# Attention and mixture of experts in one kernel: gate weights and the shared expert's last rows in one stationary, the top two marked in place, part of the residual on other engines

## The reference, cut to what matters

```python
xn = layernorm(x)                                  # x: 16 x 256 x 128
# attention, per sequence
w = exp(tanh(((xn @ W + b) @ xn.T) / (|i - j| + 1e-7)))   # diagonal set to zero
attn = (w / (sum(w, -1) + 1e-7)) @ xn
# experts, per token: 8 experts, 2 taken, hidden size 176
scores = sigmoid(xn @ gate_w.T)
_, sel = top_k(scores + expert_bias, 2)
# routed input is xn * score of the expert taken
routed = sum over sel of square(relu(score * xn @ w_up[e].T)) @ w_down[e].T
shared = square(relu(xn @ shared_w_up.T)) @ shared_w_down.T
out = x + attn + routed + shared
```

## Time and profile before

| what | value |
|---|---|
| time, median of 3 runs | 129.37 us (129.23 to 129.52) |
| the profiled execution | 129.49 us, of which the span from first to last instruction is 127.6 |
| TensorE, matmul / weight load | 116.4 us (91%) / 84.6 us (66%), 960 instructions each |
| VectorE | 109.9 us (86%), 331 instructions |
| ScalarE | 82.5 us (65%), 106 instructions |
| GpSimd | 63.8 us (50%), 114 instructions |
| chain that ended last | PE 79%, DVE 11%, DMA 3%, issue 2%, ACT 2%, POOL 1% |
| granted TensorE clock | 0.993 over the span, 1.00 in every round |

### The profile page before, as it was taken

One profiled execution on the slowest core, in us unless ns is written; L12 is line 12 of the kernel. 1 busy time (PEld: TensorE's weight loads), 2 busy tenths in 40 slices (PEclk: granted clock), 3 DMA queues, 4 the chain that ended last, 5 costly groups with the idle time before them and its releaser, 6 DMA issues.

```text
span 127.6 us, 2805 instructions
## 1 busy us (share of the span) xinstructions
PE 116.4 (91%) x960; PEld 84.6 (66%) x960; DVE 109.9 (86%) x331; ACT 82.5 (65%) x106; POOL 63.8 (50%) x114
## 2 busy tenths in 40 slices
PE   3977787789999999999999999999999999999961
PEld 3954255457757884778567875778477856667951
DVE  5796898989999999999999999999999699968511
ACT  1226577688488927893689647983789378966400
POOL 5339719974954386437743695339643004431000
PEclk9999999999999999999999999999999999999997
DMA  3998003976666494559756866686768955698681
GB/s 86 386 406 322 12 0 43 156 145 113 113 113 116 133 177 86 99 129 115 143 97 115 189 113 113 118 181 128 99 122 133 149 107 98 155 147 169 129 213 65
DMA packets 49260, 17.65 MB, mean 138 GB/s; under 512 B 46432, under 2 KB 47200, under 8 KB 49248
## 3 DMA queue, kind: packets, MB, share of 16 engines
q1 hardware_dynamic: 48672, 15.83, 61.9%
q10 hardware_dynamic: 576, 1.66, 3.5%
HBM read 3.85 MB, written 2.10 MB: 47 GB/s over the span
## 4 chain that ended last, share of the span: by engine, by line
PE 79%; DVE 11%; DMA 3%; issue 2%; ACT 2%; POOL 1%; POOLq 0%; ACTq 0%
PE h_ps L633 14%; PE out_ps L659 12%; PE dots L587 10%; PE side L604 10%; DVE gated L467 6%; PE out_ps L651 6%; PE side L616 4%; PE small L579 4%; PE out_ps L666 4%; PE out_ps L648 4%; PE small L560 3%; DMA hiddenT<-hidden 3%; PE side L621 3%; PE small L568 2%; DVE resid L479 1%
## 5 line engine op out<-in xcount | busy, mean ns | idle before, releaser
L341 ACT ACTIVATE hidden<-gated 128x1408 bf16<-128x1408 bf16 x32 | 43.9, 1376 | 17.3 <-DVE gated L467 17.3
L467 DVE SCALAR_TENSOR_TENSOR gated<-h_ps,gates 128x1408 bf16<-128x1408 f32 x32 | 51.6, 1613 | 3.2 <-PE h_ps L633 3.2
L633 PE MATMUL h_ps<-upT,xnTb 128*128 128x512 bf16 (+1 forms) x96 | 24.3, 362 | 1.5 <-DVE gated L467 1.5
L225 POOL TENSOR_SCALAR xn<-x_sb,meanvar,rstd 128x128 f32<-128x128 f32 x28 | 22.0, 800 | 0.6
L659 PEld LDWEIGHTS out_ps<-downT,hiddenT 128*128 128x128 bf16 x308 | 19.4, 98 | 3.3
L659 PE MATMUL out_ps<-downT,hiddenT 128*128 128x128 bf16 x308 | 21.4, 219 | 0.0
L258 POOL TENSOR_TENSOR shidden<-srelu 128x512 f32<-128x512 f32 (+1 forms) x16 | 13.2, 828 | 15.4 <-ACT srelu L335 15.3
L251 POOL TENSOR_SCALAR_AFFINE_SELECT probs<-probs 128x256 f32<-128x256 f32 x16 | 6.6, 410 | 26.2 <-ACT probs L329 26.2
L587 PE MATMUL dots<-projT,xnT 128*128 128x256 f32 x60 | 16.4, 396 | 1.7 <-ACT projT L320 1.5
L604 PE MATMUL side<-xn,probs 128*128 128x129 f32 x128 | 17.0, 275 | 0.6 <-DVE resid L479 0.6
L604 PEld LDWEIGHTS side<-xn,probs 128*128 128x128 f32 x128 | 16.0, 192 | 2.1 <-issue 1.3
(11 more groups left out here) (84 smaller groups left out, 152.1 us busy)
## 6 DMA issues: line engine op xcount, KB each, us to landing
x_sb<-in_x SPq DMA_DIRECT2D x7, 256.0 KB, 9.1
out_y<-final SPq DMA_DIRECT2D x7, 256.0 KB, 2.6
up_raw<-in_up ACTq DMA_DIRECT2D x1, 704.0 KB, 7.0
down_raw<-in_down ACTq DMA_DIRECT2D x1, 704.0 KB, 9.0
hiddenT<-hidden SPq DMA_TRANSPOSE x32, 3.5
out_y<-final SPq DMA_DIRECT2D x2, 128.0 KB, 1.9
late_sb<-in_late SPq DMA_DIRECT2D x1, 224.0 KB, 7.1
x_sb<-in_x ACTq DMA_DIRECT2D x1, 128.0 KB, 2.8
```

Of the source, the lines that this page charges most:

```text
L225: g.tensor_scalar(xn[:, c, t, 0:D], x_sb[:, c, t, :], meanvar[:, c % 2, t, 0:1], rstd[:, c % 2, t:t + 1], ALU.subtract, ALU.mult).then_inc ...
L341: a.activation(hidden[:, t, :], gated[:, t, :], ACT.Square).then_inc(squared, 1)
L467: v.scalar_tensor_tensor(out=gated[:, t, :].rearrange("p (e h) -> p e h", e=E), in0=h_ps[:, 0:NH].rearrange("p (e h) -> p e h", e=E), scal ...
L633: last = t_.matmul(h_ps[:, at:to], xnTb[:, c % 4, t * P:(t + 1) * P], upT[:, at:to], start=True, stop=True)
```

## The change

- The gate's 8 columns and the shared expert's last 48 rows of weights stand together in one 64-column stationary, `restT`. `rest(f)` multiplies it in two matmuls with 256 tokens each, in the place of `logits(f)`; `shared_tail` is gone. Rows 0 to 7 and 64 to 71 of the result are logits, the 48 behind each are the tail of the shared expert of the front chunk.
- ScalarE takes exp of all rows (256 columns, its scale a column `gate_sign` that is -1 in the logits' rows and 0 elsewhere), then relu of the same rows (`relu_rest`); GpSimd squares that (`square_rest`). `transpose_exp` makes two transposes and also waits for the relu; in chunk 0 it writes to `h_ps`, so the first up-projection waits until they are read.
- The top two: the two largest values are copied to `pair`, whose other places hold a large negative number; `match_replace` writes a mark where the biased scores equal one of them; one operation on VectorE compares with the mark and multiplies by the scores. `max_index`, the two comparisons, GpSimd's two products and the table of expert numbers are gone.
- The residual of each chunk's first sequence: ScalarE scales attention by its norm (`scale_attention`), GpSimd adds x (`add_x`). The second sequence's stays on VectorE.
- Orders: on TensorE `up_tile(c,2)` stands ahead of `down_tile(o,1)`; on VectorE the sums, the norm, the statistics and the routing are interleaved anew; on ScalarE and GpSimd the new steps stand as in the diff. Semaphores count accordingly.
- The transfer of early constants has 32 columns more, that of late ones 64 fewer.

```diff
-W_AT, GATE_AT, B_AT, EB_AT, EARLY = 0, D, D + 32, D + 33, D + 33 + E
-SUP_AT, SDOWN_AT, STAIL_AT, LATE = 0, 192, 192 + D, 192 + D + D
+W_AT, REST_AT, B_AT, EB_AT, EARLY = 0, D, D + 64, D + 65, D + 65 + E
+SUP_AT, SDOWN_AT, STAIL_AT, LATE = 0, P, P + D, P + D + D
...
+        expneg = sb("expneg", [P, S])
...
+        def exp_bank(c):
+            return small[:, S:2 * S] if c else h_ps[:, 0:S]
...
-            def make_gates(c):
-                pool.wait_ge(match_ready, c + 1)
-                g.tensor_tensor(chosen[:, :, :], match[:, 0, :, :], match[:, 1, :, :], ALU.add).then_inc(gate_step, 1)
-                pool.wait_ge(gate_step, c + 1)
-                wait(pool, h_taken, TILES * (c - 1))
-                g.tensor_tensor(gates[:, c % 2, :, :], chosen[:, :, :], scores[:, :, :], ALU.mult
-                                ).then_inc(gates_ready, 1)
...
-            def square_shared(c, part):
-                pool.wait_ge(sup_taken, 2 * c + part + 1)
+            def square_shared(c):
+                pool.wait_ge(sup_taken, c + 1)
                 wait(pool, out_made, TILES * (c - 1))
-                cols = slice(0, CH) if part == 0 else slice(CH, CH + S)
-                g.tensor_tensor(shidden[:, c % 2, cols], srelu[:, c % 2, cols], srelu[:, c % 2, cols], ALU.mult
+                g.tensor_tensor(shidden[:, c % 2, :], srelu[:, c % 2, :], srelu[:, c % 2, :], ALU.mult
                                 ).then_inc(sup_squared, 1)
+
+            def add_x(c):
+                pool.wait_ge(attn_scaled, c + 1)
+                wait(pool, final_ready, c - 1)
+                g.tensor_tensor(resid[:, c % 2, 0:2, :], scaled[:, c % 2, :, :], x_sb[:, c, 0:2, :], ALU.add
+                                ).then_inc(first_resid, 1)
+
+            def square_rest(c):
+                pool.wait_ge(rest_taken, c + 1)
+                wait(pool, out_made, TILES * (c - 3))
+                g.tensor_tensor(rest_hidden[:, c % 4, :], rest_relu[:, c % 2, :], rest_relu[:, c % 2, :], ALU.mult
+                                ).then_inc(rest_squared, 1)
...
                         rsqrt(k + 1)
                         normalize(k + 1)
-                    square_shared(c, 0)
-                if 1 <= f < NCH:
-                    make_gates(f)
+                    if f < NCH:
+                        square_rest(f)
+                    add_x(c)
+                    square_shared(c)
                 if f < NCH:
                     mask(f, 0)
-                if c >= 0:
-                    square_shared(c, 1)
+                if f == 0:
+                    square_rest(0)
                 if f < NCH:
                     mask(f, 1)
...
             def exp_logits(c):
-                act.wait_ge(logits_made, c + 1)
+                act.wait_ge(rest_made, c + 1)
+                if c == 0:
+                    act.wait_ge(sign_set, 2)
                 wait(act, expT_made, c)
-                a.activation(expneg[:, :], small[:, 0:P], ACT.Exp, scale=-1.0).then_inc(logits_taken, 1)
+                a.activation(expneg[:, :], small[:, 0:S], ACT.Exp, scale=gate_sign[:, :]).then_inc(logits_taken, 1)
+
+            def relu_rest(c):
+                act.wait_ge(rest_made, c + 1)
+                wait(act, rest_squared, c - 1)
+                a.activation(rest_relu[:, c % 2, :], small[:, 0:S], ACT.Relu).then_inc(rest_taken, 1)
...
+            def scale_attention(c):
+                act.wait_ge(attn_step, 2 * Q * c + 2)
+                wait(act, first_resid, c - 1)
+                for t in range(2):
+                    last = a.activation(scaled[:, c % 2, t, :], side[:, t * (D + 1):t * (D + 1) + D], ACT.Identity,
+                                        scale=rownorm[:, 0, t:t + 1])
+                last.then_inc(attn_scaled, 1)
...
+            relu_rest(0)
             cast_up()
             for k in range(0, NCH):
                 f, c = k, k - 1
                 if f >= 1:
+                    scale_attention(c)
                     exp_logits(f)
+                    relu_rest(f)
                     square(c, 0)
                     square(c, 1)
                     take_proj(f)
                 if f >= 2:
-                    relu_shared(c, 0)
+                    relu_shared(c)
                 if f >= 1:
                     square(c, 2)
                 take_tanh(f, 0)
                 take_exp(f, 0)
                 if f == 0:
-                    relu_shared(0, 0)
-                if f >= 2:
-                    relu_shared(c, 1)
+                    relu_shared(0)
                 if f + 1 < NCH:
                     take_xT(f + 1)
                 if f >= 1:
                     square(c, 3)
                 take_tanh(f, 1)
                 take_exp(f, 1)
-                if f == 0:
-                    relu_shared(0, 1)
...
+            relu_shared(LAST)
+            scale_attention(LAST)
+            for t in range(TILES):
+                square(LAST, t)
...
+            def route_one(c):
+                dve.wait_ge(expT_made, c + 1)
+                v.tensor_scalar(onep[:, :, :].rearrange("p (h i) e -> p i h e", h=2),
+                                exp_bank(c).rearrange("p (i h n) -> p i h n", i=2, h=2)[:, :, :, 0:E],
+                                1.0, None, ALU.add).then_inc(expT_taken, 1)
+
             def route_scores(c):
-                dve.wait_ge(expT_made, c + 1)
-                v.tensor_scalar(onep[:, :, :], small[:, 0:P].rearrange("p (t e) -> p t e", t=TILES)[:, :, 0:E],
-                                1.0, None, ALU.add).then_inc(expT_taken, 1)
                 dve.wait_ge(expT_taken, c + 1)
                 wait(dve, gates_ready, c)
                 v.reciprocal(scores[:, :, :], onep[:, :, :]).then_inc(topk_step, 1)
+
+            def route_bias(c):
...
             def route_top(c):
                 then(c, 2)
                 for t in range(TILES):
-                    v.max(top8[:, t, :], biased[:, t, :]).then_inc(topk_step, 1)
-
-            def route_index(c):
+                    v.max(top8[:, t, :], biased[:, t, 0:E]).then_inc(topk_step, 1)
+
+            def route_pair(c):
                 then(c, 6)
+                v.tensor_copy(pair[:, :, 0:2], top8[:, :, 0:2]).then_inc(topk_step, 1)
+
+            def route_mark(c):
+                then(c, 7)
                 for t in range(TILES):
-                    v.max_index(top8_at[:, t, :], top8[:, t, :], biased[:, t, :]).then_inc(topk_step, 1)
-
-            def route_match(c):
-                if c == 0:
-                    dve.wait_ge(iota_e_made, 1)
-                then(c, 10)
-                wait(dve, gate_step, c)
-                experts = iota_e[:, :].rearrange("p (t e) -> p t e", t=1).to_broadcast([P, TILES, E])
-                for j in range(2):
-                    last = v.tensor_tensor(match[:, j, :, :], experts,
-                                           top8_at[:, :, j:j + 1].to_broadcast([P, TILES, E]), ALU.is_equal)
-                last.then_inc(match_ready, 1)
+                    v.match_replace(marked[:, t, 0:E + 6], pair[:, t, :], biased[:, t, 0:E + 6], MARK
+                                    ).then_inc(topk_step, 1)
+
+            def route_gates(c):
+                then(c, K)
+                wait(dve, h_taken, TILES * (c - 1))
+                v.scalar_tensor_tensor(out=gates[:, c % 2, :, :], in0=marked[:, :, 0:E], scalar=MARK,
+                                       in1=scores[:, :, :], op0=ALU.is_equal, op1=ALU.mult).then_inc(gates_ready, 1)
...
-            def attend(c, q):
+            def attend_sums(c, q):
                 dve.wait_ge(attn_made, Q * c + q + 1)
+                if q == 0:
+                    wait(dve, attn_scaled, c)
                 sums = side[:, 0:2 * (D + 1)].rearrange("p (t n) -> p t n", t=2)[:, :, D]
                 v.tensor_scalar(rowsum[:, q, :], sums, ATT_EPS, None, ALU.add).then_inc(attn_step, 1)
+
+            def attend_norm(c, q):
                 dve.wait_ge(attn_step, 2 * (Q * c + q) + 1)
                 v.reciprocal(rownorm[:, q, :], rowsum[:, q, :]).then_inc(attn_step, 1)
-                dve.wait_ge(attn_step, 2 * (Q * c + q) + 2)
+
+            def attend(c):
+                dve.wait_ge(attn_step, 2 * (Q * c + 1) + 2)
                 for t in range(2):
                     last = v.scalar_tensor_tensor(
-                        out=resid[:, c % 2, 2 * q + t, :], in0=side[:, t * (D + 1):t * (D + 1) + D],
-                        scalar=rownorm[:, q, t:t + 1], in1=x_sb[:, c, 2 * q + t, :],
+                        out=resid[:, c % 2, 2 + t, :], in0=side[:, t * (D + 1):t * (D + 1) + D],
+                        scalar=rownorm[:, 1, t:t + 1], in1=x_sb[:, c, 2 + t, :],
                         op0=ALU.mult, op1=ALU.add)
                 last.then_inc(attn_taken, 1)
...
                 mid = c >= 0
                 if c >= 1:
                     gate(c, 0)
+                if mid:
+                    attend_sums(c, 0)
+                    attend_norm(c, 0)
```

(98 more changed lines are left out.)

64 lines of the change are left out of this document (28 added, 36 removed).

## The result

The changed kernel takes 128.62 us (median of 4 runs, 128.46 to 128.68) against 129.34 for the kernel before (4 runs): a ratio of 0.9941, 95% interval 0.9926 to 0.9956. That is 0.7 us less, where I forecast 1.2 (128.2, range 127.2 to 129.4). The profiled span went from 127.6 to 126.9 us.

The account below looks back on a forecast made before the run. TensorE's chain of pieces was taken to bound the steady rounds. Start +0.4, six rounds x -0.25 = -1.5 and drain -0.1 gave -1.2 us: 128.2 against the median of 129.37, range 127.2 to 129.4.

Parts of the forecast that it names:

- Pieces of the round: TensorE, steady round: tail -0.58, rest +0.22, second transpose of exp +0.11, transposes of x -0.15; 13.62 becomes 13.22 us.
- the 0.15: TensorE, each round: transposes of x fall from 0.59 to 0.44 once no 64-column tail stands ahead of them.
- The estimate of 0.43: TensorE, `rest` free of tiling-mode drains: 0.43 instead of 0.58, total another 0.9 us lower; not used in the sum.
- The new wait: TensorE, up(c,2) waits for the bank that gate(c,1) reads: 0.15 late, round 13.37, gain 0.25.
- VectorE and the routing: VectorE, steady round: removed and added operations net 13.05 to 12.2 us, leaving 1.1 us of slack in 13.37.
- GpSimd: GpSimd, each round: loses two gate products (0.5), gains add_x (0.61); mask(f,0) ends a microsecond before attention needs it, so covered.
- The start: Start, up to up(1,0): later transposes of exp and gate(0,2) move it from 27.49 to 27.9, +0.4 (bounds +0.1 and +0.9).
- The drain: Last round and drain: last gate ends 10.15 after up(LAST,0) starts, against 10.25; -0.1 (bounds -0.5 and +0.3).
- A round without the stall (13.22): Rival, TensorE rounds: no wait at up(c,2), 6 x 0.15 = 0.9 better, 127.3; chance 0.10.
- stay at 0.59: Rival, transposes of x and last round's dots keep their cost (+0.9), start +0.3: 129.4, no change; chance 0.15.
- ScalarE's head: Rival, another wait, above all at the head of ScalarE's round, over 0.5 late every round: 129.7 to 131; chance 0.06.
- match_replace as a bound: Rival, VectorE's routing: match_replace slow; at 0.45 an instruction the kernel takes 131.4; chance 0.05.

Follow-up runs that it names:

- the orders mended: Changed kernel with down_tile(o,1) ahead of up_tile(c,2) again and, in round 1, GpSimd's mask ahead of its squaring: 127.03 us, 0.9820 of the kernel before.
- the mended order: Changed kernel with only down_tile(o,1) put back ahead of up_tile(c,2) on TensorE: 127.41 us, 0.9843 of the kernel before.

## Why the prediction was right, point by point

- *The bound.* Right. Rounds are TensorE's pieces plus one hand-over, at granted clock 1.00.
- *Pieces of the round.* `rest` 0.58 (forecast 0.58), transposes of exp 0.23 (0.23), transposes of x 0.44 to 0.45 (0.44), tail gone. The row from the start, which was the only ground for the 0.15, held in every round. The Trainium skill's rule that a change of the tiling mode drains TensorE (TensorEngine Tiling (Array Packing), Key Properties) agrees with it, though no run separates a drain from another cause. The estimate of 0.43 for a `rest` without such drains was not reached: the trace has 0.58.
- *The new wait.* Right in kind and nearly in size: up(c,2) 0.17 late instead of 0.15. The profile has VectorE waiting 0.73 for up(c,1) there (I had 0.5), so the gate did start at once:

```profile
59.53 1.62 DVE L498 SCALAR_TENSOR_TENSOR gated<-h_ps,gates 128x1408 bf16<-128x1408 f32 x1 [0.73 <-PE h_ps L681]
```

- *The term left out.* project right behind the down-projection costs 0.91; it was 0.86 behind the up-projection. The sum had no row for it. Together with the 0.02 of the wait and roundings the round is 13.46 instead of 13.37: 0.5 us in six rounds. The six rounds are thus the mis-sized term of the sum: forecast -1.5, and -1.0 measured from the end of the first attention group to up(LAST,0) (29.67 to 108.51 against 29.13 to 109.02). That is about the difference between 128.2 and 128.62. The start, 0.14 dearer, and the drain, 0.12 cheaper, cancel by luck.
- *VectorE and the routing.* match_replace 0.158 (forecast 0.16). The copy of the pair was forecast at 0.15 and takes 0.69 in a round, where it ends with GpSimd's addition (64.85 and 64.81); with that addition gone it took 0.67 and ended with the squaring of the tail, so it is not that addition in particular. The product of the gates takes 0.41 and ends with the mask, 0.4 as the prediction had it for this case (its sum had 0.25). VectorE is therefore busy for 12.61 of a round instead of the forecast 12.2. Both were covered:

```profile
64.09 0.72 POOL L263 TENSOR_TENSOR resid<-scaled,x_sb 128x256 f32<-128x256 f32 x1
64.16 0.69 DVE L470 COPY pair<-top 128x8 f32<-128x8 f32 x1
...
64.96 0.16 DVE L475 MATCH_REPLACE8 marked<-pair,biased 128x14 f32<-128x14 f32 x1
```

The Trainium skill (SBUF — State Buffer, Who interferes with whom) lists a copy among the operations that can enter a mode with both ports and so contend with GpSimd, when its operands allow it. The 0.69 agrees. I had used the rule for the start, where the copy took 0.28, and for the product, and not for the copy in a round. What I missed altogether is that the routing's length still matters while VectorE has slack: with the orders mended, comparisons held up by GpSimd made the round 0.13 longer.
- *ScalarE.* Scaling 0.36, exp 0.47, relu 0.39, and the transpose of exp waits for nothing in a round. Right.
- *GpSimd.* In a round right, though add_x takes 0.72 instead of 0.61; in the start wrong. "mask(f,0) ends a microsecond before attention needs it" was read from a steady round and applied to round 1, where cast_down stands ahead and normalization is late. Attention (1,0) waited for the mask, and with it ahead of the squaring the kernel is 0.5% faster.
- *The start.* Forecast +0.4 by way of VectorE, until up(1,0), which came at 27.71, +0.22 (+0.16 counted from the first statistics). After it came the wait for the mask, so that the attention behind it ended 0.54 later than before. The size was near, the reason half of it another.
- *The drain.* gate(LAST,0) started 1.0 after up(LAST,0) began (forecast 1.1), and the last gate ended 10.0 after it (forecast 10.15; 116.92 + 1.62 less 108.51).
- *The rivals.* A round without the stall (13.22) was not what happened, but it is what the mended order gives: 13.24. The transposes of x did not stay at 0.59, ScalarE's head came late in no steady round, and there is no sign of match_replace as a bound. The range held, but the measured gain, 0.59%, is two thirds of the forecast 0.9%.

## What to carry to other kernels

Where one engine's pieces fill a round, count the pieces, and for each bank handed to and fro add the other engine's operation and both hand-overs, then see what lies between: moving a tile up in the queue can take away the very work that covered it. Slack of an engine over a round says little; ask at what moment it reaches the one operation that another waits for. And a part that relieves an engine with slack can still cost in the start and the drain, where the chain runs along other engines, so read the order of those stages by themselves.

## What the runs showed of the hardware

- A copy of 8 elements on VectorE takes 0.16 to 0.72 us, the gates' product of 32 elements 0.18 to 1.03, two comparisons 0.29 to 1.18. The long ones end just after an operation of GpSimd: the copy at 64.85 after the addition at 64.81, the product at 68.00 after the mask at 67.95, which has a single input. The product of 1.02 sat through the rest of a squaring and a whole mask (28.50 after 28.45). The bias with two SBUF inputs stayed at 0.19 beside GpSimd's normalization in every steady round, so not each pairing excludes; why, was not tried.
- An fp32 matmul of 512 columns (project, two records) took 0.91 us right behind the bf16 down-projection (records of 592 to 648 ns) and 0.86 behind the bf16 up-projection (592 ns each). The cause was not tried.
- VectorE's first statistics started between 3.50 and 3.91 us in the profiled executions, when x had landed. Stages were therefore compared from that point on.
